# Edge attention pass of a fused graph transformer: per-tile sums kept in two PSUM banks instead of folding the SBUF accumulator into every item

## The chip, the cores and the metric

One core of one Trainium2 chip. The metric is the device time of one execution of the whole program, in microseconds, as the median of several runs.

## The reference, cut to what matters

The program runs a whole two-layer model on 3125 nodes and 100000 edges. The change lies in the edge attention of the second layer:

```python
def _edge_attention(xn, edge_index, ef, ew, Wq, bq, Wk, bk, Wv, bv, We, be, Wo, bo):
    n = xn.shape[0]
    scale = DH ** (-0.5)
    q = (xn @ Wq + bq).reshape(n, H, DH)
    k = (xn @ Wk + bk).reshape(n, H, DH)
    v = (xn @ Wv + bv).reshape(n, H, DH)
    src, dst = (edge_index[0], edge_index[1])
    ep = ef @ We + be
    scores = jnp.einsum('ehd,ehd->eh', q[dst], k[src] + ep[:, None, :]) * scale
    scores = scores * ew[:, None]
    m = jax.ops.segment_max(scores, dst, num_segments=n)
    m = jnp.where(jnp.isfinite(m), m, 0.0)
    ex = jnp.exp(scores - m[dst])
    s = jax.ops.segment_sum(ex, dst, num_segments=n)
    attn = ex / s[dst]
    out = jax.ops.segment_sum(attn[:, :, None] * v[src], dst, num_segments=n)
    out = out.reshape(n, D) @ Wo + bo
    return out
```

H is 8 heads and DH is 32. `dst` is sorted, so the edges of one node, and of one tile of 128 nodes, stand together.

## The kernel before

The edges are cut into 416 items of 256 edges; all edges of an item end in the same tile of 128 nodes (25 tiles), and a table `sh.tile_id` says which. `stage_flash` takes 8 items at a time: one window, 52 windows in all, each of four groups of two items. The loop is software-pipelined: one pass of `body(s, a, ffn)` works on the scores of window `s` (the next one) and on the sums of window `a` (the one before it), and on a piece of an unrelated feed-forward (`ffn`) that fills TensorE. Every engine runs its own written-out list in order; semaphores tie them together. No planner is involved.

For window `s` and each group `g`:

- GpSimd gathers the key and value rows of the edges (`store<-kv_d`, L2816) into a ring of two windows; it may overwrite a group's rows only when `sums_done` says that the sums of two windows before are through.
- ScalarE's `place(s, g)` makes the one-hot matrix `mem_t` in two passes (L2945, L2948); TensorE's `ask(s, g)` multiplies it with the queries into the one `query` bank pair (L2840, 8 instructions of 256 columns: each fp32 product is two instructions). VectorE's `add` (L3038), `mult` (L3045) and `reduce` (L3049) turn this into scores, and `scale` (L3055) ends the window. `ask(s, g)` waits for `mult(s, g-1)`, since `query` is a single buffer.

For window `a`:

- TensorE turns the scores (L2868), VectorE scans them for the running maxima (`within`, L3065 on; `across`, L3075 on), with small TensorE products in between (L2884, L2890), then TensorE turns the result back (L2901, L2902) and ScalarE takes the exponential (L2985).
- VectorE's `rescale` (L3105) multiplies the accumulator of the window's first tile by the fall of the maximum, and `weigh(a, g)` (L3110) multiplies the value rows by the weights.
- ScalarE's `belong(a, g)` (L2954, L2957) makes the one-hot matrices `member`; TensorE's `collect(a, n)` (L2853) sums item `n` into one of three PSUM banks, `n % 3`, with four instructions of 264 columns.
- TensorE's `fold(a, n)` (L2860) then adds the SBUF accumulator of the item's tile by a product with the identity, two instructions of 264 columns. ScalarE's `keep(a, n)` (L2963) copies the bank back to the accumulator. `fold(n)` waits for `keep(n-1)`; `collect` itself waits for a `keep` only in items 0 and 1.

In the text, A0 to A3 are `ask(s, 0)` to `ask(s, 3)`, and C0 to C3 the collecting of the items 2g and 2g+1 of window `a`. TensorE's list before, from the middle of a pass, is A1, items 0, 1, 2, 3 with the folds of 0 to 2, A2, fold 3, items 4, 5 with fold 4, A3, fold 5, items 6, 7 with their folds. ScalarE's list there is keep 0, place 2, keep 1, belong 2, keep 2, place 3, keep 3, belong 3, keep 4, place 0 of the next window, keep 5 to 7.

Of the kernel before, what the change touches and what calls it, by code (L numbers as in the profile page):

```python
# [319 lines left out]
def stage_edge_tables(nc, sh):  # L320

    with ExitStack() as ctx:
# [65 lines left out]
        with nc.Block() as block:  # L388
            @block.sync
            def _(sp):  # L390
# [8 lines left out]
                sp.dma_start(sh.tile_id[:, 0:NI], sh.tile_d.rearrange("(a i) -> a i", a=1)).then_inc(ids_in, 16)  # L399
# [2249 lines left out]
def stage_flash(nc, sh, w1, w2, b1):  # L2649
# [6 lines left out]
    with ExitStack() as ctx:  # L2656
# [42 lines left out]
        pa = sb("pa", [P, P + H])  # L2699
        query = ps("query", [P, 4 * D])  # L2700
# [40 lines left out]
        down_added = sem("down_added")  # L2741

        def tile_numbers(eng, w):

            _, values = nc.values_load_multi_w_load_instructions(
                sh.tile_id[0:1, bass.ds(WI * w.at, WI)], engines=[eng.engine], min_val=0, max_val=NT - 1,
                skip_runtime_bounds_check_because="the table was clamped to 0 .. NT - 1 when it was made")
            return values
# [13 lines left out]
        with nc.Block() as block:  # L2762
# [62 lines left out]
            def _(pe):  # L2825
# [18 lines left out]
                def collect(a, n):  # L2844

                    g = n // 2
                    pe.wait_ge(member_ready, G * a.at + (g + 1))
                    pe.wait_ge(pv_ready, G * a.at + (g + 1))
                    if n < 2:
                        pe.wait_ge(added, WI * a.at + (n + 1))  # L2850
                    for k in range(SUBS):
                        c = n % 2 * SUBS + k
                        pe.matmul(sums[:, n % 3, 0:W], member[:, g % 2, c, :], ring[:, a.side * WS + 4 * g + c, HI_],  # L2853
                                  start=(k == 0), stop=False)

# [706 lines left out]
```

## Time and profile before

| what | value |
|---|---|
| median of 3 runs | 3732.68 us (3732.53 to 3735.69) |
| profiled execution, its own time | 3734.78 us |
| its span | 3733.0 us |
| mean granted TensorE clock | 0.878 |
| edge attention pass (`stage_flash`) | about 1900 to 3227 us of the span |

The profile is of one execution. "Busy" of TensorE counts pipelined matmuls with modelled ends, so rows of several matmuls give the time from the first start to the last end; the time that a group really takes from the engine is the distance from its start to the start of the next group. PE is TensorE, PEld its weight loads, DVE VectorE, ACT ScalarE, POOL GpSimd.

### The profile page before, as it was taken

The page shows a single profiled execution, that of the slowest core. Times are in us where ns is not written, and L with a number is a line of the kernel's source. Part 1 is how long each engine was busy: PE and PEld are TensorE (multiplying, and loading weights), DVE is VectorE, ACT ScalarE, POOL GpSimd, SP SyncE. Part 2 cuts the span into 40 slices and gives each one's busy share as a digit, 9 for nine tenths or more (in the row PEclk, how much of TensorE's full clock was granted, in tenths as well). Part 3 has the DMA queues.
Part 4 walks back from the last instruction along what each step waited for, and adds up shares of the span by engine and source line. Part 5 has one row for each costly group of instructions (what it writes and reads, how often), then busy time and mean ns, then how long its engine had stood idle before and what let it go on. Part 6 is the DMA issues. An engine that isn't in the chain of part 4 may idle for free. (4 is left out here: it accounts for less than half of the span.)

```text
span 3733.0 us, 52272 instructions
## 1 busy us (share of the span) xinstructions
PE 3127.7 (84%) x13504; PEld 2408.8 (65%) x13504; DVE 2161.4 (58%) x4835; ACT 1687.2 (45%) x3903; POOL 1888.5 (51%) x1845
## 2 busy tenths in 40 slices
PE   2778888788878689769859999999999999659798
PEld 2567666566665578646437777777777777436565
DVE  6333334333334600075569999999999999653515
ACT  1444333333334122233246676667676676332323
POOL 2777777777772044401046666666666666120010
PEclk8778767777778599979769999999999999779899
DMA  5555555555550167641067777777777777300000
GB/s 143 148 147 146 139 153 140 154 144 142 147 141 20 44 192 218 182 167 63 9 190 218 222 219 218 214 224 218 218 216 221 221 219 209 111 24 1 22 5 35
DMA packets 345535, 547.29 MB, mean 147 GB/s; under 512 B 170928, under 2 KB 222389, under 8 KB 344967
## 3 DMA queue, kind: packets, MB, share of 16 engines
q0 software_dynamic: 113216, 348.74, 32.8%
q1 hardware_dynamic: 224312, 183.42, 16.8%
q10 hardware_dynamic: 7743, 12.07, 1.0%
q8 instruction: 111, 1.82, 0.2%
q14 instruction: 153, 1.25, 0.1%
HBM read 493.32 MB, written 51.90 MB: 146 GB/s over the span
## 5 line engine op out<-in xcount | busy, mean ns | idle before, releaser
L2816 POOL DMA_INDIRECT store<-kv_d,src_of x832 | 872.4, 1049 | 414.6 <-issue 242.1
L821 POOL DMA_INDIRECT agg_rows<-xn_d,src_of x832 | 800.0, 962 | 268.7 <-issue 242.3
L993 PE MATMUL agg_sums<-agg_rows,agg_member 128*128 128x257 f32 x1664 | 578.0, 501 | 181.7 <-DVE acc L885 92.4
L834 ACT ACTIVATE agg_rows<-agg_rows,weight_of 128x256 f32<-128x256 f32 x832 | 373.0, 500 | 632.1 <-DMA agg_rows<-xn_d,src_of 631.5
L993 PEld LDWEIGHTS agg_sums<-agg_rows,agg_member 128*128 128x128 f32 x1664 | 387.7, 249 | 323.9 <-DVE acc L885 130.0
L885 DVE TENSOR_TENSOR acc<-acc,agg_sums 128x257 f32 x416 | 176.3, 424 | 598.9 <-PE agg_sums L993 598.0
L2840 PE MATMUL flash_query<-q,flash_mem_t 128*128 x1664 | 411.7, 391 | 48.3 <-DVE store L3045 37.7
L2853 PE MATMUL flash_sums<-store,flash_member 128*128 128x264 f32 x1664 | 422.8, 387 | 2.2 <-DVE store L3110 2.2
L2840 PEld LDWEIGHTS flash_query<-q,flash_mem_t 128*128 128x128 f32 x1664 | 312.7, 193 | 100.9 <-issue 54.6
L2853 PEld LDWEIGHTS flash_sums<-store,flash_member 128*128 128x128 f32 x1664 | 317.1, 191 | 56.1 <-issue 2.2
L3045 DVE TENSOR_TENSOR store<-store,flash_query 128x1024 f32<-128x1024 f32 x208 | 252.3, 1213 | 39.3 <-PE flash_query L2840 39.0
L2963 ACT ACTIVATE acc<-flash_sums 128x264 f32 x416 | 159.3, 383 | 252.2 <-PE flash_sums L2860 251.8
L2860 PE MATMUL flash_sums<-acc,ident 128*128 x832 | 269.2, 405 | 2.1 <-ACT acc L2963 1.6
L983 PEld LDWEIGHTS agg_edge<-agg_we,agg_feats 65*128 65x128 f32 x1664 | 249.7, 230 | 23.8 <-issue 10.4
L2954 ACT ACTIVATE flash_member<-lane,lane_of 128x128 f32<-128x128 f32 x832 | 264.1, 395 | 0.1
L3038 DVE TENSOR_TENSOR store<-store,flash_ep 128x1024 f32<-128x1024 f32 x208 | 252.5, 1214 | 9.9 <-DMA flash_ep<-ep_d 9.5
L3110 DVE TENSOR_TENSOR store<-store,flash_pa 128x1056 f32<-128x1056 f32 x208 | 255.7, 1251 | 0.0
L983 PE MATMUL agg_edge<-agg_we,agg_feats 65*128 65x32 f32 x1664 | 239.8, 304 | 11.6 <-DMA agg_feats<-in_ef_t_dram 11.0
L3049 DVE TENSOR_REDUCE flash_dots<-store 128x32 f32<-128x1024 f32 x208 | 247.8, 1211 | 1.8
L2860 PEld LDWEIGHTS flash_sums<-acc,ident 128*128 128x128 f32 x832 | 145.4, 189 | 64.3 <-issue 48.7
L876 DVE TENSOR_SCALAR agg_member<-lane,lane_of 128x128 f32<-128x128 f32 x832 | 175.8, 300 | 10.1 <-issue 1.5
L1649 DVE TENSOR_TENSOR moe_y<-moe_down,moe_b 128x512 f32<-128x512 f32 x32 | 22.1, 692 | 244.9 <-PE moe_down L1508 244.9
(468 smaller groups left out, 4574.3 us busy)
## 6 DMA issues: line engine op xcount, KB each, us to landing
moe_w<-in_L_ffn_W_dram SPq DMA_DIRECT2D x64, 512.0 KB
agg_feats<-in_ef_t_dram SPq DMA_DIRECT2D x104, 256.0 KB, 4.4
flash_goal<-goal_d SPq DMA_DIRECT2D x52, 512.0 KB, 4.4
agg_rows<-xn_d,src_of POOLq DMA_INDIRECT x832, 2.8
ep_d<-agg_ep SPq DMA_DIRECT2D x52, 256.0 KB
store<-kv_d,src_of POOLq DMA_INDIRECT x832, 4.1
flash_ep<-ep_d SPq DMA_DIRECT2D x416, 32.0 KB
flash_flags<-flags_d SPq DMA_DIRECT2D x416, 32.0 KB
```

The costliest lines, as they stand in the source:

```text
L821: pool.indirect_dma_start(rows[:, q, 0:D], None, sh.xn_d, bass.IndirectOffsetOnAxis(ap=sh.src_of[:, c:c + 1], axis=0)).then_inc(gathered[u ...
L834: act.activation(rows[:, q, 0:D], rows[:, q, 0:D], ACT.Copy, scale=sh.weight_of[:, bass.ds((UI * i + u) * SUBS + k, 1)]).then_inc(weighted, 1)
L983: last = pe.matmul(edge[:, p, c * DH:(c + 1) * DH], feats[:, p, c * P:(c + 1) * P], we_s[:, :], start=True, stop=True)
L993: last = pe.matmul(sums[:, j % 4, 0:W], member[:, c % (2 * BI * SUBS), :], rows[:, c % NB, :], start=(c % SUBS == 0), stop=(c % SUBS == SU ...
L2816: pool.indirect_dma_start(ring[:, s, :], None, sh.kv_d, bass.IndirectOffsetOnAxis(ap=sh.src_of[:, c:c + 1], axis=0)).then_inc(gathered[p][ ...
L2840: last = pe.matmul(query[:, c * D:(c + 1) * D], mem_t[:, g % 2, c * P:(c + 1) * P], sh.q[:, bass.ds(t, 1), :], start=True, stop=True)
L2853: pe.matmul(sums[:, n % 3, 0:W], member[:, g % 2, c, :], ring[:, a.side * WS + 4 * g + c, HI_], start=(k == 0), stop=False)
L2860: pe.matmul(sums[:, n % 3, 0:W], sh.ident[:, :], sh.acc[:, bass.ds(tiles[n], 1), :, :].rearrange("p a h v -> p (a h v)"), start=False, sto ...
L2954: act.activation(member[:, g % 2, k, :], sh.lane[:, :], ACT.Abs, scale=-1.0, bias=sh.lane_of[:, bass.ds(WS * a.at + (4 * g + k), 1)])
L3038: dve.tensor_tensor(r, r, ep[:, s.side, 4 * g:4 * g + 4, :].unsqueeze(2).to_broadcast([P, 4, H, DH]), ALU.add).then_inc(add_done, 1)
L3045: dve.tensor_tensor(r, r, query[:, :].rearrange("p (k f) -> p k f", k=4), ALU.mult).then_inc(mult_done, 1)
L3110: dve.tensor_tensor(r, r, e.unsqueeze(3).to_broadcast([P, 4, H, VW]), ALU.mult).then_inc(pv_ready, 1)
```

## The change

The two items of a group are summed straight into a running sum that stays in PSUM. Bank 1 or 2 of `sums` belongs to a tile, by turns (`bank_id`); the next tile takes the other bank. There is no fold. Where an item is the first of its tile, its bank must first forget what it holds: a product of one row and one column of zeros (`clear_l`, `clear_r`, bf16) with `start=True` goes to column 511 of the bank that `open_id` names; where the item is not the first, `open_id` is 0 and the product goes to the unused bank 0. `keep` still copies the bank to the SBUF accumulator after every item, `rescale` now works on the PSUM bank, and VectorE makes both tables from `tile_id` at the start of the stage. The order of the calls on TensorE and ScalarE and their waits change too.

```diff
-                def collect(a, n):
-
-                    g = n // 2
+                def collect(a, g, banks, opened):
                     pe.wait_ge(member_ready, G * a.at + (g + 1))
                     pe.wait_ge(pv_ready, G * a.at + (g + 1))
-                    if n < 2:
-                        pe.wait_ge(added, WI * a.at + (n + 1))
-                    for k in range(SUBS):
-                        c = n % 2 * SUBS + k
-                        pe.matmul(sums[:, n % 3, 0:W], member[:, g % 2, c, :], ring[:, a.side * WS + 4 * g + c, HI_],
-                                  start=(k == 0), stop=False)
-
-                def fold(a, n, tiles):
-
-                    pe.wait_ge(rescaled, a.at + 1)
-                    pe.wait_ge(added, WI * a.at + (n + 2))
-                    pe.matmul(sums[:, n % 3, 0:W], sh.ident[:, :],
-                              sh.acc[:, bass.ds(tiles[n], 1), :, :].rearrange("p a h v -> p (a h v)"),
-                              start=False, stop=True).then_inc(sums_done, 1)
+                    if g == 0:
+                        pe.wait_ge(rescaled, a.at + 1)
+                    if WI * a.at + 2 * g > 0:
+                        pe.wait_ge(added, WI * a.at + 2 * g)
+                    for n in (2 * g, 2 * g + 1):
+                        pe.matmul(sums[:, bass.ds(opened[n], 1), 511:512].rearrange("p a w -> p (a w)"), clear_l[:, :], clear_r[:, :],
+                                  start=True, stop=True)
+                        for k in range(SUBS):
+                            c = n % 2 * SUBS + k
+                            last = pe.matmul(running(banks[n]), member[:, g % 2, c, :], ring[:, a.side * WS + 4 * g + c, HI_],
+                                             start=False, stop=(k == SUBS - 1), skip_group_check=True)
+                        last.then_inc(sums_done, 1)
...
-                        tiles = tile_numbers(pe, a)
-                        collect(a, 0)
-                        fold(a, 0, tiles)
-                        collect(a, 1)
-                        fold(a, 1, tiles)
-                        collect(a, 2)
-                        collect(a, 3)
-                        fold(a, 2, tiles)
+                        banks, opened = bank_numbers(pe, a), open_numbers(pe, a)
+                        collect(a, 0, banks, opened)
                     if s is not None:
                         ask(s, 2, ask_tiles)
                     if a is not None:
-                        fold(a, 3, tiles)
-                        collect(a, 4)
-                        collect(a, 5)
-                        fold(a, 4, tiles)
+                        collect(a, 1, banks, opened)
                     if s is not None:
                         ask(s, 3, ask_tiles)
                     if a is not None:
-                        fold(a, 5, tiles)
-                        collect(a, 6)
-                        fold(a, 6, tiles)
-                        collect(a, 7)
-                        fold(a, 7, tiles)
+                        collect(a, 2, banks, opened)
+                        collect(a, 3, banks, opened)
+                    else:
+                        pe.wait_ge(banks_ready, 1)
...
-                def keep(a, n, tiles):
-                    act.wait_ge(sums_done, WI * a.at + (2 * WI + n + 1))
+                def keep(a, n, tiles, banks):
+                    act.wait_ge(sums_done, WI * a.at + (2 * WI + n // 2 * 2 + 2))
+                    if n % 2 == 1:
+                        act.wait_ge(added, WI * a.at + n)
                     act.activation(sh.acc[:, bass.ds(tiles[n], 1), :, :].rearrange("p a h v -> p (a h v)"),
-                                   sums[:, n % 3, 0:W], ACT.Copy).then_inc(added, 1)
+                                   running(banks[n]), ACT.Copy).then_inc(added, 1)
...
-                        keep(a, 3, tiles)
+                        keep(a, 3, tiles, banks)
                         belong(a, 3)
-                        keep(a, 4, tiles)
                     if more:
                         place(after(s), 0)
                     if a is not None:
-                        for n in range(5, WI):
-                            keep(a, n, tiles)
+                        for n in range(4, WI):
+                            keep(a, n, tiles, banks)
...
-                dve.sem_inc(added, 2)
...
-                def rescale(a, tile):
+                def rescale(a, bank):
                     dve.wait_ge(exp_ready, a.at + 2)
-                    dve.wait_ge(added, WI * a.at + 2)
-                    r = sh.acc[:, bass.ds(tile, 1), :, :].rearrange("p a h v -> p (a h) v")
+                    if a.at > 0:
+                        dve.wait_ge(added, WI * a.at)
+                    r = running(bank).rearrange("p (h v) -> p h v", h=H)
```

TensorE's list in one pass, from the last product of the turn back (`flash_diag`) on; `flash_query` is the output of an ask and `flash_sums` that of a collect or a fold. Before:

```order
L2902 MATMUL flash_small<-flash_diag,flash_first_hot 128x8
L2840 ISA
L2840 MATMUL flash_query<-q,flash_mem_t 128x256 x2
L2840 ISA
L2840 MATMUL flash_query<-q,flash_mem_t 128x256 x2
L2745 TENSOR_LOAD tile_id
L2853 MATMUL flash_sums<-store,flash_member 128x264 x2
L2860 ISA
L2860 MATMUL flash_sums<-acc,ident 128x264
L2853 MATMUL flash_sums<-store,flash_member 128x264 x2
L2860 ISA
L2860 MATMUL flash_sums<-acc,ident 128x264
```

The same place now, as far as the start of A2:

```order
L2917 MATMUL flash_small<-flash_diag,flash_first_hot 128x8
L2859 ISA
L2859 MATMUL flash_query<-q,flash_mem_t 128x256 x2
L2859 ISA
L2859 MATMUL flash_query<-q,flash_mem_t 128x256 x2
L2752 TENSOR_LOAD tile_id x2
L2871 ISA
L2871 MATMUL flash_sums<-flash_clear_r,flash_clear_l 128x1
L2875 ISA
L2875 MATMUL flash_sums<-store,flash_member 128x264 x2
```

Two products of a collect and one of a fold have become one clearing product and two of a collect, each behind a register instruction (ISA), and a second table is read (TENSOR_LOAD). What follows the second item moved most: A2 stood behind four items, it now stands behind two, and A3 behind four in place of six.

VectorE's list at the start of the stage has these rows new, behind the last one that it had there before:

```order
L3040 CAST flash_member<-tile_id 1x416
L3041 MEMSET flash_hidden 1x1
L3042 MEMSET flash_member 1x416
L3044 TENSOR_TENSOR flash_hidden<-flash_member 1x415
L3046 SCALAR_TENSOR_TENSOR flash_member<-flash_hidden,flash_member 1x416
L3048 CAST tile_id<-flash_member 1x416
L3050 TENSOR_SCALAR tile_id<-tile_id 1x416
L3052 CAST flash_member<-tile_id 1x416
L3054 TENSOR_SCALAR flash_member<-flash_member 1x416
L3056 TENSOR_TENSOR flash_hidden<-flash_hidden,flash_member 1x416
L3057 CAST tile_id<-flash_member 1x416
L3059 CAST tile_id<-flash_hidden 1x416
```

They run once and stand ahead of the first `add`, where nothing stood before; a clearing of the three `sums` banks also joins the memsets ahead of them.

## Rows read from the trace of the kernel before

**Rows 1.** The page: span in 40 slices, TensorE, VectorE and granted clock.

```profile
PE   2778888788878689769859999999999999659798
...
DVE  6333334333334600075569999999999999653515
...
PEclk8778767777778599979769999999999999779899
```

**Rows 2.** Busy time by stretch, one of 260 us in the pass.

```profile
2220.00:2480.00 260.00, 247.88 (x1177) 200.24 (x1176) 241.48 (x366) 180.68 (x433) 175.47 (x167) 1.00 0.75 218
```

**Rows 3.** VectorE's waits between 1960 and 3200 us: total, times, longest.

```profile
DVE store L3045 <- PE flash_query L2840: 32.7, 51, 1.1
DVE flash_run L3075 <- PE flash_small L2884: 16.0, 50, 0.3
```

**Rows 4.** Timeline of one window: start, us, engine, line, count, idle before.

```profile
2503.09 1.89 PE L2840 MATMUL flash_query<-q,flash_mem_t 128*128 x8
...
2504.81 0.61 PE L2860 MATMUL flash_sums<-acc,ident 128*128 x2
...
2505.26 1.21 DVE L3045 TENSOR_TENSOR store<-store,flash_query 128x1024 f32<-128x1024 f32 x1
...
2508.20 0.32 PE L2868 MATMUL flash_small<-ident,flash_scaled 128*128 128x128 f32 x1
...
2508.35 1.96 PE L2877 MATMUL flash_up<-flash_xt,store 128*128 128x128 f32 x16
...
2509.13 0.41 DVE L3065 TENSOR_TENSOR_SCAN flash_ahead<-flash_flags,flash_small 128x128 f32<-128x128 f32 x1
...
2510.53 0.23 PE L2884 MATMUL flash_small<-flash_z,flash_row_head 128*8 128x32 f32 x2 [0.21 <-DVE flash_z L3070]
...
2514.92 1.21 DVE L3045 TENSOR_TENSOR store<-store,flash_query 128x1024 f32<-128x1024 f32 x1
...
2516.38 1.99 PE L2840 MATMUL flash_query<-q,flash_mem_t 128*128 x8 [0.68 <-DVE store L3045]
...
2518.21 1.05 PE L2853 MATMUL flash_sums<-store,flash_member 128*128 128x264 f32 x4
...
2519.10 0.61 PE L2860 MATMUL flash_sums<-acc,ident 128*128 x2
...
2519.84 0.39 ACT L2963 ACTIVATE acc<-flash_sums 128x264 f32 x1 [1.86 <-PE flash_sums L2860]
...
2520.87 0.72 ACT L2948 ACTIVATE flash_mem_t<-flash_mem_t,ones 128x512 f32<-128x512 f32 x1
...
2523.24 1.89 PE L2840 MATMUL flash_query<-q,flash_mem_t 128*128 x8
...
2525.24 1.22 DVE L3045 TENSOR_TENSOR store<-store,flash_query 128x1024 f32<-128x1024 f32 x1 [0.62 <-PE flash_query L2840]
```

**Rows 5.** The page: the group of the folds, all windows.

```profile
L2860 PE MATMUL flash_sums<-acc,ident 128*128 x832 | 269.2, 405 | 2.1 <-ACT acc L2963 1.6
```

**Rows 6.** Timeline of an earlier stage, around a matmul of one column.

```profile
1704.05 0.28 PE L2170 MATMUL mid_zsum<-ones,mid_kr 128*128 128x1 f32 x2
1704.19 0.68 PE L2168 MATMUL mid_zsum<-store,mid_kr 128*128 128x256 f32 x2
```

**Rows 7.** The table read: duration ns, first and last start.

```profile
L2745 PEldq TENSOR_LOAD <-tile_id x104: 587/591/634, 1909.2 to 3208.2; - x104
```

**Rows 8.** VectorE at the start of the pass (timeline), and an operation on 257 elements (page).

```profile
1917.97 2.36 DVE L3038 TENSOR_TENSOR store<-store,flash_ep 128x1024 f32<-128x1024 f32 x2 [9.53 <-DMA flash_ep<-ep_d]
...
L885 DVE TENSOR_TENSOR acc<-acc,agg_sums 128x257 f32 x416 | 176.3, 424 | 598.9 <-PE agg_sums L993 598.0
```

**Rows 9.** TensorE at its slower clock: by stretch, and twice in the timeline.

```profile
460.00:720.00 260.00, 212.62 (x867) 164.63 (x867) 98.06 (x340) 97.39 (x227) 197.83 (x205) 0.74 0.56 150
...
515.56 2.05 PE L993 MATMUL agg_sums<-agg_rows,agg_member 128*128 128x257 f32 x4 [2.28 <-issue]
...
1931.50 3.62 PE L2840 MATMUL flash_query<-q,flash_mem_t 128*128 x8 [2.67 <-DVE store L3045]
```

More of the change, by code:

```diff
@@ L2741, in stage_flash, with numbers, bank_numbers, open_numbers @@
         down_added = sem("down_added")
-        def tile_numbers(eng, w):
[L2745 to L2748, printed above, removed]
+        banks_ready = sem("banks_ready")
+        def numbers(eng, w, table, least, most):
+            _, values = nc.values_load_multi_w_load_instructions(
+                table[0:1, bass.ds(WI * w.at, WI)], engines=[eng.engine], min_val=least, max_val=most,
+                skip_runtime_bounds_check_because="the table was made on the chip within these bounds")
+            return values
+        def tile_numbers(eng, w):
+            return numbers(eng, w, sh.tile_id, 0, NT - 1)
+        def bank_numbers(eng, w):
+            return numbers(eng, w, bank_id, 1, 2)
+        def open_numbers(eng, w):
+            return numbers(eng, w, open_id, 0, 2)
+        def running(bank):
+            return sums[:, bass.ds(bank, 1), 0:W].rearrange("p a w -> p (a w)")
         def after(s):
@@ L2982, in body @@
                         belong(a, 0)
-                        tiles = tile_numbers(act, a)
+                        tiles, banks = tile_numbers(act, a), bank_numbers(act, a)
                         act.wait_ge(back_ready, a.at + 1)
@@ L2986, in body @@
                         belong(a, 1)
-                        keep(a, 0, tiles)
+                        keep(a, 0, tiles, banks)
                     if s is not None:
@@ L2990, in body @@
                     if a is not None:
-                        keep(a, 1, tiles)
+                        keep(a, 1, tiles, banks)
                         belong(a, 2)
-                        keep(a, 2, tiles)
+                        keep(a, 2, tiles, banks)
                     if s is not None:
@@ L3002, in body @@
                     if a is not None:
-                        for n in range(5, WI):
-                            keep(a, n, tiles)
+                        for n in range(4, WI):
+                            keep(a, n, tiles, banks)
+                    else:
+                        act.wait_ge(banks_ready, 1)
                 windows(act, body)
@@ L3009, in _ @@
             def _(dve):
-                dve.sem_inc(added, 2)
                 dve.sem_inc(down_added, 1)
+                dve.memset(clear_l[:, :], 0.0)
+                dve.memset(clear_r[:, :], 0.0)
+                dve.memset(sums[:, :, :], 0.0)
                 dve.memset(sh.acc[:, :, :, :], 0.0)
@@ L3028, in _ @@
                 dve.drain().then_inc(heads_ready, 1)
+                dve.tensor_copy(turns, sh.tile_id[0:1, :])
+                dve.memset(opens[:, 0:1], 1.0)
+                dve.memset(none, 0.0)
+                dve.drain()
+                dve.tensor_tensor(opens[:, 1:NI], turns[:, 1:NI], turns[:, 0:NI - 1], ALU.not_equal)
+                dve.drain()
+                dve.tensor_tensor_scan(turns, opens, none, 0.0, ALU.add, ALU.max)
+                dve.drain()
+                dve.tensor_copy(bank_id[:, :], turns)
+                dve.drain()
+                dve.tensor_scalar(bank_id[:, :], bank_id[:, :], 1, None, ALU.bitwise_and)
+                dve.drain()
+                dve.tensor_copy(turns, bank_id[:, :])
+                dve.drain()
+                dve.tensor_scalar(turns, turns, 1.0, None, ALU.add)
+                dve.drain()
+                dve.tensor_tensor(opens, opens, turns, ALU.mult)
+                dve.tensor_copy(bank_id[:, :], turns)
+                dve.drain()
+                dve.tensor_copy(open_id[:, :], opens)
+                dve.drain().then_inc(banks_ready, 1)
                 def key_rows(s, g):
```

14 lines of the change are left out of this document (10 added, 4 removed).

## Prediction

> **What bounds the kernel now.** The slices say where the change lies: TensorE and VectorE are both at 9 tenths for the whole edge pass, about a third of the span, and the granted clock is full there, which it is hardly anywhere else for so long [rows 1]. A stretch inside the pass says how near both are: 247.9 and 241.5 us busy of 260 [rows 2]. So neither can win much without the other. VectorE's waits tell who waits for whom: 32.7 us of its idle time end with an ask (`mult` waits for the query product), 51 times, and 16.0 us with the small product L2884 [rows 3]. That is 0.64 and 0.32 us of each window. The timeline then gives one period: from `mult` 2 at 2525.24, back over its wait of 0.62 us for A2, to `mult` 0 at 2514.92, whose end lets A1 start. Behind A1, TensorE has four items and three folds before A2 [rows 4]. The loop that sets the time is thus `mult` 0, A1, collects and folds, A2, `mult` 2, VectorE's list, `mult` 0. The same `mult` 2 stood at 2500.69 one window earlier (2525.24 less the 24.55 us that I take as the period; 51 such periods make up the pass).
>
> **What goes.** A window has 16 fold instructions of 264 columns (832 in all [rows 5]). A collect of four starts at 2518.21 and its fold at 2519.10 [rows 4], so one instruction takes 0.2225 us of TensorE, and the folds 3.56 us of the window.
>
> **What comes.** Eight clearing products a window, each with its own weights and one column. The nearest row is L2170: two instructions of one column in an earlier stage go from 1704.05 to the next at 1704.19, so 0.07 us each [rows 6], the lower bound. Above stands 0.23, the whole of the small pair L2884 from first start to last end; half of it, 0.12, is what one of two such products takes with a start of its own [rows 4]. A register instruction now stands ahead of each, so I take c = 0.12 us rather than 0.07: 0.96 a window. The second table read takes 0.59 us on TensorE's sequencer [rows 7]; it is issued while A1's 1.83 us run, and two of 0.59 still fit, so I cost it at nothing (0.6 us a window if that cover were gone). `rescale` keeps its 264 elements; PSUM or SBUF, `add` and `mult` differ by nothing in the rows (1.22 and 1.21 us), so nothing. By TensorE's load alone the window would shrink by 3.56 - 0.96 = 2.60 us.
>
> The tables: 11 operations on 416 elements of one row. An operation on 257 takes 0.42 us, so 416 take about 0.7, and the scan, 0.41 for 128 elements [rows 4], at most 1.3; with the PSUM memset some 9 to 10 us. VectorE sits idle 9.53 us before its first `add` [rows 8]. Cost 0 to 1 us, once; I take 0.
>
> **What moves: the waits.** This is where I expect the time. `collect` of group g now waits for every earlier `keep`, and `keep` waits for the whole pair. Between the asks this makes one chain that hands over between TensorE and ScalarE. I follow it from `mult` 0 (time 0 = 2514.92), with three lengths from [rows 4]: an ask holds TensorE 1.73 us (2503.09 to 2504.81); a pair of items needs 1.05 + 0.89 = 1.94 us to its last end and holds TensorE 1.78, each plus 2c; from that end to `keep` there are 0.13 us (2519.71 to 2519.84).
> - A1 starts at 1.46 and C0 at 3.29, as now. C0 ends at 5.23 + 2c. `keep` 0 starts at 5.36 + 2c. `place` 2 stands behind it and is ready 1.75 later (2519.84 to 2520.87 + 0.72), at 7.11 + 2c; A2 starts at 7.24 + 2c, in place of 8.32. So A2 comes 0.84 us earlier and `mult` 2's wait of 0.62 goes.
> - C1 starts at 8.97 + 2c and ends at 10.91 + 4c. `keep` 2 was through before A2's end; now it waits for C1, and `place` 3 behind it: 12.79 + 4c. A3 starts at 12.92 + 4c, in place of 12.72 (2503.09 is one period earlier). TensorE is idle for about 2.2 us. `mult` 3 follows at 14.92 + 4c against 14.89 (2505.26): the whole gain at `mult` 2 is given back.
> - C2 starts at 14.65 + 4c, ends at 16.59 + 6c. `keep` 4 starts at 16.72 + 6c, `keep` 5 must wait for it, 0.43, and ends at 17.54 + 6c. C3 waits for `keep` 5: 17.67 + 6c, and TensorE is idle 1.1 us again.
> - The turn L2868 stands behind C3: 19.45 + 8c. Now it stands at 17.83 (2508.20). It is 1.62 + 8c late.
> - Next late is L2884. VectorE's list reaches it 1.40 after L3065, which can start some 0.38 after the turn; TensorE has 16 instructions of the feed-forward between (2508.35 to 2510.31) and gets to it about 2.15 us after the turn, now 2.33. So it is late by 1.44 + 8c, and from there to the next `mult` 0 the list is VectorE's and does not change.
>
> With c = 0.12 a window is 2.40 us longer, with 0.07 2.00 and with 0.23 3.28. Times 51: 122 us (102 to 167). GpSimd is not behind this: its 16 gathers of about 1.3 us need 21 us of what is then 27.
>
> **The clock.** The pass has the full clock now. The stage with the lower mean, 0.74, has TensorE idle in pieces of one to two us between its groups [rows 9]; four instructions behind an idle piece of 2.28 us took 2.05 us there, where the pass needs 1.05 for four. In the pass itself, an ask behind 2.67 us of idle time took 3.62 us, against 1.99 [rows 9, 4]. The new window has two idle pieces of about 2.2 us (before A2 and before A3) and one of 1.1. So I expect the lower of the two levels (1.2 in place of 2.4 GHz) now and then: one group of eight a window at 3.62 in place of 1.99, 1.63 us, and since TensorE is on the chain nearly all the way, all of it counts: 83 us. Bounds: nothing, and two groups a window, 166 us.
>
> The Trainium skill ("TensorE: Matmul & The Clock Gate", the section on a second failure mode, PSUM-queue depth cycling) speaks against this change in the same way: a kernel that cycles through PSUM banks and leaves TensorE small idle pieces between groups goes back and forth between the two levels. By that rule the pass would lose its full clock; by the slice row alone (1.00 throughout) one would add nothing. The rows of the earlier stage agree with the rule.
>
> **The sum.** The profiled execution took 3734.78 us, span 3733.0, the runs' median 3732.68: they agree within 0.1%, so I add to the median. 3732.7 + 122 + 83 = 3938 us.
>
> **The rivals.**
> - *Chain without clock loss.* The hand-overs cost as worked out, but the pieces of 2.2 us are too short to lower the clock: 3855 us (3835 to 3900 by c). For it: the pass has idle pieces of 0.7 us every window and stays at 1.00. Against: the rows at 2.28 and 2.67 us. Chance 0.33; the forecast with clock loss has 0.43.
> - *More is lost.* Two groups or more a window at the lower clock, or c above 0.3: 4021 us and more. Chance 0.07 beyond 4040.
> - *The gain at A2 stands* (other side). If `place` 3 did not end up behind C1, that is if A3 could start by 12.72 - 0.62 = 12.1 and C3 could follow C2 without a stop, `mult` 2's wait is all that changes: 51 times 0.62, 32 us, so 3701 us; VectorE's whole wait for TensorE, 50 us, would be the floor, 3683. It decides at the point where `keep` 2 and `keep` 4, 5 cost TensorE less than the 2.6 us that the folds free. For it: TensorE's load falls by 2.6 us. Against: ScalarE's list has `keep` 2 ahead of `place` 3, and C1 is behind A2. Chance 0.12.
> - *Nothing to be seen.* The two cancel within 0.2%: 0.03. A small loss up to 3825: 0.02.
>
> **How the numbers follow.** The likeliest is 3938 us. The range goes from the chain with the smallest c and no clock loss, 3835, rounded down to 3825, to two groups a window plus a little, 4035; it leaves out the other side and the excess. About 0.2% (7.5 us) is what a measurement of this kernel can tell from no change. Faster 0.12, same 0.03, slower 0.85.
>
> **What would show it.** In the changed profile: the waits of TensorE for `keep` (ACT acc) and `place` (ACT flash_mem_t) new, of about 1 and 2 us, once and twice a window; VectorE waiting about 1 us or more for L2868 or L2884 and for A3, and no longer for A2; a window of 27 to 29 us; TensorE's instructions of the pass fewer by 416; the granted clock of the pass below 1.00. I am wrong in the chain if A3 does not wait for `place` 3; wrong in the clock term if the pass keeps 1.00; wrong in c if a pair of items holds TensorE much more or less than 2.0 us.

## The result, and the profile after

The change makes the kernel slower: 4036.14 us (median of 4 runs, 4033.61 to 4038.53) against 3732.61 us before (3731.63 to 3735.69, 4 runs). The ratio is 1.0811 [1.0797, 1.0825], a loss of 303.5 us. The forecast was 3938 us with a range of 3825 to 4035 us, so the time lies 1 us above the range and 98 us above the forecast.

The page of the changed kernel, its slices (to be held against [rows 1]), and two groups of its part 5:

```profile
PE   2888878888885996895778778877877787649888
...
DVE  6323333433345001746777777777777777562524
...
PEclk8777777877785998996899999999999999869999
...
L2859 PE MATMUL flash_query<-q,flash_mem_t 128*128 x1664 | 500.8, 453 | 255.2 <-ACT flash_mem_t L2953 217.5
...
L2871 PEld LDWEIGHTS flash_sums<-flash_clear_r,flash_clear_l 1*128 1x128 bf16 x416 | 38.0, 91 | 245.0 <-issue 245.0
```

TensorE and VectorE, both at 9 tenths in the edge pass before, are both at 7 to 8 tenths now: neither of them bounds the pass any longer; they wait for something. The busy times of the same stretch as in [rows 2] say it in microseconds (TensorE, its weight loads, VectorE, ScalarE, GpSimd, then the granted clock): TensorE has 42 us less of 260, VectorE 43 less, and the granted clock is 0.93:

```profile
2220.00:2480.00 260.00, 206.16 (x874) 145.41 (x872) 198.85 (x299) 143.29 (x345) 140.09 (x135) 0.93 0.61 175
```

The waits of VectorE and TensorE between 2000 and 3450 us (total, times, longest) name it. Against [rows 3], VectorE's wait for an ask has grown from 32.7 to 192.7 us, twice a window, and a wait for the turn (L2883, L2868 before) is new. TensorE in turn waits for `place` (L2953) twice a window and for `keep` (L2970) once:

```profile
DVE store L3077 <- PE flash_query L2859: 192.7, 94, 4.4
DVE flash_ahead L3097 <- PE flash_small L2883: 105.5, 47, 2.5
...
PE flash_query L2859 <- ACT flash_mem_t L2953: 192.7, 94, 2.1
PE flash_sums L2871 <- ACT acc L2970: 66.1, 47, 1.4
```

The timeline of one window (the changed kernel, 2517 to 2544 us) shows the chain, from the last part of one pass into the next (start, duration, engine, line, count, idle before):

```profile
2517.66 0.39 ACT L2970 ACTIVATE acc<-flash_sums  x1 [1.07 <-PE flash_sums L2875]
...
2518.26 0.39 ACT L2970 ACTIVATE acc<-flash_sums  x1 [0.21 <-ACT acc L2970]
...
2518.91 0.17 PE L2871 MATMUL flash_sums<-flash_clear_r,flash_clear_l 1*128 1x1 bf16 x1 [1.41 <-ACT acc L2970]
...
2521.22 0.27 PE L2883 MATMUL flash_small<-ident,flash_scaled 128*128 128x128 f32 x1
...
2521.59 0.42 DVE L3097 TENSOR_TENSOR_SCAN flash_ahead<-flash_flags,flash_small 128x128 f32<-128x128 f32 x1 [2.43 <-PE flash_small L2883]
...
2527.47 1.21 DVE L3077 TENSOR_TENSOR store<-store,flash_query 128x1024 f32<-128x1024 f32 x1
...
2528.94 1.99 PE L2859 MATMUL flash_query<-q,flash_mem_t 128*128 x8 [0.68 <-DVE store L3077]
...
2531.07 0.17 PE L2871 MATMUL flash_sums<-flash_clear_r,flash_clear_l 1*128 1x1 bf16 x1
...
2532.27 0.09 PEld L2871 LDWEIGHTS flash_sums<-flash_clear_r,flash_clear_l 1*128 1x128 bf16 x1 [0.34 <-issue]
2532.27 0.17 PE L2871 MATMUL flash_sums<-flash_clear_r,flash_clear_l 1*128 1x1 bf16 x1
2532.37 0.74 PEld L2875 LDWEIGHTS flash_sums<-store,flash_member 128*128 128x128 f32 x4
2532.38 1.16 PE L2875 MATMUL flash_sums<-store,flash_member 128*128 128x264 f32 x4
...
2533.69 0.39 ACT L2970 ACTIVATE acc<-flash_sums  x1 [3.16 <-PE flash_sums L2875]
...
2534.72 0.72 ACT L2953 ACTIVATE flash_mem_t<-flash_mem_t,ones 128x512 f32<-128x512 f32 x1
...
2535.58 3.65 PE L2859 MATMUL flash_query<-q,flash_mem_t 128*128 x8 [2.05 <-ACT flash_mem_t L2953]
...
2541.78 0.39 ACT L2970 ACTIVATE acc<-flash_sums  x1 [4.10 <-PE flash_sums L2875]
...
2543.67 1.99 PE L2859 MATMUL flash_query<-q,flash_mem_t 128*128 x8 [2.05 <-ACT flash_mem_t L2953]
```

Read from 2531.07 on: C0 ends, `keep` 0 starts, `place` 2 follows, and only then A2, after 2.05 us in which TensorE has nothing. A2 itself takes 3.65 us instead of the 1.99 of a group of eight at the full clock. The same hand-over comes again between C1 and A3 (2541.78 to 2543.67), and a smaller one between C2 and C3, at the top.

The length of a window is best read from turn to turn, the first and the last of the 52 turns. Before, of two timelines of L2868:

```profile
1938.17 0.33 PE L2868 MATMUL flash_small<-ident,flash_scaled 128*128 128x128 f32 x1 [3.04 <-DVE flash_scaled L3055]
...
3202.58 0.28 PE L2868 MATMUL flash_small<-ident,flash_scaled 128*128 128x128 f32 x1
```

After, of L2883:

```profile
1937.74 0.30 PE L2883 MATMUL flash_small<-ident,flash_scaled 128*128 128x128 f32 x1 [3.09 <-issue]
...
3503.95 0.27 PE L2883 MATMUL flash_small<-ident,flash_scaled 128*128 128x128 f32 x1
```

That is 1264.41 us for 51 periods before, 24.79 each, and 1566.21 now, 30.71 each. The pass accounts for 301.8 of the 303.5 us; outside it nothing moved. The setup of the tables on VectorE stayed in its idle time, as predicted: the first turn is even 0.4 us earlier.

### The profile page after: what moved, and what is told of

Its sections match the earlier page's. It is cut to its first block and busy times, and to the rows that moved or that the text cites. A ratio compares the mean times of both kernels' runs of the same rounds, so it can differ in the third digit from the quotient of the medians.

```text
span 4036.8 us, 51618 instructions
## 1 busy us (share of the span) xinstructions
PE 3180.7 (79%) x13088; PEld 2331.4 (58%) x13088; DVE 2177.5 (54%) x4850; ACT 1687.8 (42%) x3903; POOL 1882.3 (47%) x1845
## 5 line engine op out<-in xcount | busy, mean ns | idle before, releaser
L2859 PE MATMUL flash_query<-q,flash_mem_t 128*128 x1664 | 500.8, 453 | 255.2 <-ACT flash_mem_t L2953 217.5
L2859 PEld LDWEIGHTS flash_query<-q,flash_mem_t 128*128 128x128 f32 x1664 | 350.3, 221 | 358.2 <-issue 303.3
L2875 PE MATMUL flash_sums<-store,flash_member 128*128 128x264 f32 x1664 | 500.4, 425 | 0.3
L2970 ACT ACTIVATE acc<-flash_sums x416 | 160.3, 385 | 613.6 <-PE flash_sums L2875 591.3
L2875 PEld LDWEIGHTS flash_sums<-store,flash_member 128*128 128x128 f32 x1664 | 294.6, 197 | 39.0 <-issue 0.2
L2871 PEld LDWEIGHTS flash_sums<-flash_clear_r,flash_clear_l 1*128 1x128 bf16 x416 | 38.0, 91 | 245.0 <-issue 245.0
L2962 ACT ACTIVATE flash_member<-flash_member,ones 128x512 f32<-128x512 f32 x208 | 150.1, 722 | 14.3
```

The source lines that it names most:

```text
L2859: last = pe.matmul(query[:, c * D:(c + 1) * D], mem_t[:, g % 2, c * P:(c + 1) * P], sh.q[:, bass.ds(t, 1), :], start=True, stop=True)
L2875: last = pe.matmul(running(banks[n]), member[:, g % 2, c, :], ring[:, a.side * WS + 4 * g + c, HI_], start=False, stop=(k == SUBS - 1), sk ...
```

## Experiments

Below, "the length of a window" is always taken as above, from the first to the last turn, divided by 51, and the "quiet" length is the lower quartile of the 51 periods (24.59 us in the kernel before). "Slow asks" are groups of eight of L2859 (L2840 in the kernel before) of over 2.1 us in place of 1.99, counted from the first to the last turn; the kernel before has 2 of them, the changed kernel has 62, of which 49 are an A2. All traces are of one execution each.

### First set

Four kernels went to a chip on which the kernel before took 4408.72 us itself. The traces there show stops of some 10 us in which ScalarE and VectorE stand still together, for instance in the timeline of the first of them:

```profile
2840.37 1.14 ACT L2985 ACTIVATE flash_hidden<-flash_up,flash_b 128x128 f32<-128x128 f32 x4 [9.42 <-DMA xn_d<-store]
2840.41 0.23 DVE L3107 TENSOR_TENSOR_SCAN flash_run<-flash_steps,flash_run,flash_small 8x16 f32<-8x16 f32 x1 [10.39 <-remote]
```

The times of this set (4591.11, 4545.97, 4557.58 and 4593.78 us) are therefore no measure, and three of the four were run again on another chip. Their expectations:

The places ahead of the keeps in ScalarE's list:

> ScalarE makes place 2 and place 3 ahead of keep 0 and keep 2; nothing else changes. Theory H (hand-overs): the two idle pieces of TensorE of 2.05 us before A2 and A3 vanish, and with them the slower clock (A2 back from 3.65 to about 1.9 us). What stays is the 1.4 us before C3. By the durations of the changed kernel's trace the window becomes about 25.6 us in place of 30.54: 51 times 4.9 less, about 3785 us. Theory O (TensorE's own overhead, that is clearing products and register instructions, carries the loss): the same work stands on TensorE, so at most 50 us are won: 3985 us or more.

Three unused products ahead of A2 and of A3:

> Three more products of 256 columns with the identity (into the unused bank 0, 1.3 us) stand on TensorE ahead of A2 and of A3, inside the idle pieces of 2.05 us. They compute nothing that is used. Theory C (clock): TensorE's idle pieces shrink to about 0.8 us, the slower clock does not come, A2 takes 1.9 in place of 3.65 us: the kernel gets faster with more work, by 51 times 1.75 us, to about 3945 us, clock 1.00 in the pass. If the clock falls for another reason: the same 4036 us or up to 4060, since the products only fill idle time.

No clearing products:

> The eight clearing products of a window, with their register instructions, are left out, so the sums of different tiles run together (that part of the computation is missing). If each costs the 0.31 us that the changed trace shows between its start and that of its item, 2.48 us of a window go and the time is about 3910 us. If it costs the 0.12 us of the prediction, 0.96 us go: 3987 us. If other waits hide it: 4036 us.

The clearing products at a fixed address, so that no register instruction stands ahead of them:

```diff
-                        pe.matmul(sums[:, bass.ds(opened[n], 1), 511:512].rearrange("p a w -> p (a w)"), clear_l[:, :], clear_r[:, :],
-                                  start=True, stop=True)
+                        pe.matmul(sums[:, 0, 511:512], clear_l[:, :], clear_r[:, :], start=True, stop=True)
```

> The clearing products stay but go to bank 0 always, a fixed address, so the register instruction ahead of each is gone (the forgetting of the right bank is missing). If the register instruction is the cost, the time is near that of the kernel without clears (3910 us). If the product with its own weights is the cost, it is near 4036 us.

This one needs no time to be read, only the distance of two items in an undisturbed window of its timeline:

```profile
2525.01 0.17 PE L2871 MATMUL flash_sums<-flash_clear_r,flash_clear_l 1*128 1x1 bf16 x1
...
2526.19 0.09 PEld L2871 LDWEIGHTS flash_sums<-flash_clear_r,flash_clear_l 1*128 1x128 bf16 x1 [0.34 <-issue]
2526.20 0.17 PE L2871 MATMUL flash_sums<-flash_clear_r,flash_clear_l 1*128 1x1 bf16 x1
```

1.19 us from item to item, as in the changed kernel (2531.07 to 2532.27, 1.20): the computed address is not what a clearing product costs.

### The places first

ScalarE's list alone is written in another order; no work is added or removed.

```diff
                         belong(a, 1)
-                        keep(a, 0, tiles, banks)
                     if s is not None:
                         place(s, 2)
                     if a is not None:
+                        keep(a, 0, tiles, banks)
                         keep(a, 1, tiles, banks)
-                        belong(a, 2)
-                        keep(a, 2, tiles, banks)
                     if s is not None:
                         place(s, 3)
                     if a is not None:
+                        belong(a, 2)
+                        keep(a, 2, tiles, banks)
                         keep(a, 3, tiles, banks)
```

> The kernel of the run places first again, since there the kernel before took 4409 us in place of 3733, with stalls of up to 10 us of ScalarE and VectorE together that neither kernel has in the first profiles. If TensorE's two idle pieces of about 2 us and the slower clock carry the loss, as theory H says: about 3785 us beside 3733 for the kernel before, clock 1.00 in the pass. If TensorE's own overhead carries it: 3985 us or more.

Measured: 3771.99 us (3768.78 to 3776.99), ratio to before 1.0109 [1.0093, 1.0126]. Of the 303.5 us of loss 264 are gone. Its timeline at the place where the changed kernel has the hand-over:

```profile
2506.99 0.72 ACT L2953 ACTIVATE flash_mem_t<-flash_mem_t,ones 128x512 f32<-128x512 f32 x1
...
2508.02 1.16 PE L2875 MATMUL flash_sums<-store,flash_member 128*128 128x264 f32 x4
...
2509.01 1.89 PE L2859 MATMUL flash_query<-q,flash_mem_t 128*128 x8
...
2509.33 0.39 ACT L2970 ACTIVATE acc<-flash_sums  x1 [1.61 <-PE flash_sums L2875]
```

`place` 2 is through before C0 ends, A2 follows C0 with no idle time, and `keep` 0 runs beside it. The granted clock of the pass is back at full speed:

```profile
2220.00:2480.00 260.00, 227.41 (x1062) 165.79 (x1061) 233.76 (x366) 175.78 (x423) 193.84 (x165) 1.00 0.73 212
```

The window is 25.50 us long, with one slow ask. It follows that the order "keep, then place" in ScalarE's list makes most of the loss, and that the clock is lost by way of it. VectorE no longer waits for any ask between 2000 and 3200 us; what it still waits for is small products of TensorE, the turn above all, 1.28 us a window:

```profile
DVE flash_ahead L3097 <- PE flash_small L2883: 60.1, 47, 1.5
```

### Work put into the gaps

```diff
                     if s is not None:
+                        if a is not None:
+                            for n in range(3):
+                                pe.matmul(sums[:, 0, 0:D], sh.ident[:, :], sh.q[:, 0, :], start=True, stop=True)
                         ask(s, 2, ask_tiles)
```

and the same ahead of `ask(s, 3)`: twelve instructions of 256 columns more in each window, into the unused bank 0.

> The kernel with six more instructions of 256 columns ahead of A2 and of A3 again, for the same reason. Theory C (idle pieces lower the clock): about 3945 us and clock 1.00 in the pass. If the clock has another cause: 4036 to 4060 us and a slow A2 as before.

Measured: 3955.47 us (3954.23 to 3959.28), 1.0603 [1.0585, 1.0621]. With more work and nothing else changed it is 81 us faster than the changed kernel. Its timeline around A2:

```profile
2503.42 1.46 PE L2926 MATMUL flash_sums<-q,ident 128*128 128x256 f32 x6
...
2505.64 1.99 PE L2859 MATMUL flash_query<-q,flash_mem_t 128*128 x8 [0.75 <-ACT flash_mem_t L2959]
```

And the busy times and the clock of its stretch:

```profile
2220.00:2480.00 260.00, 226.77 (x1034) 165.90 (x1034) 205.26 (x318) 152.19 (x367) 151.72 (x143) 0.99 0.65 185
```

A2 still waits for `place`, but the idle piece is 0.75 us long in place of 2.05, and the ask is back at 1.99 us. One of its asks is slow in place of 62. The window is 29.08 us long, 28.73 in the quiet ones: this is the chain with the clock loss all but taken out. So the changed kernel's window of 30.71 us splits into 24.79, the chain and the clock. By the quiet length the chain makes 3.94 us and the clock 1.98; by the mean of 29.08 they make 4.29 and 1.63. The second split compares like with like, since the 24.79 is a mean too. The slow asks alone, each less 1.99, add up to 82 us, 1.6 a window.

### Without the clearing products

The product of L2871 is left out, and with it the read of the table `open_id`, which nothing on TensorE uses then (104 table reads there in place of 156). Nothing else is changed.

> The kernel without the clearing products again (the forgetting of a bank is left out). At 0.31 us each: about 3910 us. At the 0.12 us of the prediction: 3987 us.

Measured: 3866.5 us (3861.53 to 3870.45), 1.036 [1.0343, 1.0377], 170 us under the changed kernel and 44 under the lower of the two values expected. The waits of 2.05 us for `place` are all still there, so the hand-over stays. The window is 27.41 us, 26.40 in the quiet ones, and 28 asks are slow in place of 62. Against the quiet 28.73 of the kernel above, eight clearing products are worth 2.33 us, 0.29 each (some 0.1 us of the 2.33 may be the table read); the distance of two items says 0.31 (1.20 less 0.89 for four products [rows 4]). Of the 170 us some 119 are this difference (51 times 2.33); the rest goes with the fewer slow asks.

The same run closes a rival. A pair without its clears takes 1.94 us, the 1.05 + 0.89 of [rows 4], though both items now add to a running sum at a computed address:

```profile
2522.32 1.94 PE L2873 MATMUL flash_sums<-store,flash_member 128*128 128x264 f32 x8
```

So neither the shared bank nor the register address of the items costs TensorE anything here; the 0.31 us are the clear.

The 264 us of the order and the 170 us of the clears add up to more than the loss of 303.5, so they overlap. Both take in part of the clock loss, and the clears ahead of A2 and A3 can cost time only while VectorE waits for these asks.

### Three edits: places first, tables early, clears in pairs

To the reordered list come two edits on TensorE: the tables are read ahead of the wait for L2916, and both clearing products of a pair stand ahead of both items.

```diff
+                        banks, opened = bank_numbers(pe, a), open_numbers(pe, a)
                         pe.wait_ge(p_ready, a.at + 1)
...
-                        banks, opened = bank_numbers(pe, a), open_numbers(pe, a)
                         collect(a, 0, banks, opened)
...
                     for n in (2 * g, 2 * g + 1):
                         pe.matmul(sums[:, bass.ds(opened[n], 1), 511:512].rearrange("p a w -> p (a w)"), clear_l[:, :], clear_r[:, :],
                                   start=True, stop=True)
+                    for n in (2 * g, 2 * g + 1):
                         for k in range(SUBS):
```

> Places first, and two more edits: the two tables are read into TensorE's registers before the turn back instead of right ahead of C0, and both clearing products of a pair stand ahead of both items. Against places first I expect 0.3 us a window less for the tables, and 4 times 0.3 us less if the 0.31 us of a clearing product are a stop between items, which now falls once a pair: 51 times 1.5 us, about 3785 - 77 = 3708 us. If each clearing product stops the weight loads wherever it stands, only the tables gain: 3770 us.

Measured: 3751.32 us (3749.13 to 3755.64), 1.0056 [1.004, 1.0073]: 21 us better than the places alone, where 77 was hoped for. What a pair of clears costs now is in its timeline:

```profile
2502.23 0.11 PEld L2871 LDWEIGHTS flash_sums<-flash_clear_r,flash_clear_l 1*128 1x128 bf16 x2 [0.33 <-issue]
2502.23 0.20 PE L2871 MATMUL flash_sums<-flash_clear_r,flash_clear_l 1*128 1x1 bf16 x2
2502.36 2.05 PE L2876 MATMUL flash_sums<-store,flash_member 128*128 128x264 f32 x8
```

The two products go by in 0.13 us and the stop of the weight loads comes once in place of twice. Less came of it in time because VectorE is nearly the bound again (238.96 us busy of 260 in the stretch, [rows 2] has 241.48). With the places first it waited for no ask any more, so time saved ahead of A2 and A3 is not seen. Only its wait for the turn could shrink: it went from 1.28 us a window to 0.88, and the window from 25.50 to 25.14. TensorE mostly waits for VectorE:

```profile
DVE flash_ahead L3098 <- PE flash_small L2884: 43.1, 49, 2.1
...
PE flash_query L2859 <- DVE store L3078: 107.7, 96, 1.6
PE flash_sums L2871 <- ACT acc L2971: 73.1, 52, 1.4
```

One hand-over of the changed kernel is left, C3 behind `keep` 5, and it still makes VectorE wait for the turn.

### The two small edits alone, and clears of another kind

These three start from the changed kernel again. First the tables read ahead of the wait for L2916, as in the diff above:

> The changed kernel, with the two tables read into TensorE's registers ahead of the turn back, where TensorE waits for VectorE anyway, in place of right ahead of C0. If the second read holds C0 back by 0.3 us (C0 starts 3.60 us after mult 0, predicted 3.29): 51 times 0.3, about 4020 us. If it is hidden, as the prediction said: 4036 us. A shift of the idle pieces against the clock could hide or double this.

Measured: 4040.13 us (4038.93 to 4044.94), 1.082 [1.0802, 1.0838]. C0 now starts 1.92 us after A1 in 50 of 51 windows. In the changed kernel the median is 1.98 us, with single windows above 2.05, such as the one shown (2528.94 to 2531.07, 2.13). So the read held C0 up by 0.06 us as a rule, and in time that is worth nothing. The median period fell from 30.37 to 30.25 us, while 64 asks are slow in place of 62.

Then both clearing products of a pair ahead of both items, as in the diff above:

> The changed kernel, with both clearing products of a pair ahead of both items. The run with three edits shows the pair at 1.9 to 2.0 us of TensorE in place of 2.4. So four times 0.4 us a window: 51 times 1.6, about 3954 us; nothing if other waits take it up: 4036 us.

Measured: 3984.47 us (3972.53 to 3991.13), 1.0662 [1.0637, 1.0687], 52 us under the changed kernel, where 82 was hoped for. The window is 29.75 us, 28.08 in the quiet ones, with 56 slow asks. Against the quiet 28.73 with the filled gaps that is 0.65 us a window, 0.16 a pair in place of the 0.4 expected; A2 starts 6.33 us after A1 in place of 6.50 (medians). The rest of the 52 us goes with the fewer slow asks.

The third clears with full-size operands, the identity as weights and a column of zeros of 128 rows in fp32, which is two instructions:

```diff
-        clear_r = sb("clear_r", [1, 1], BF16)
+        clear_r = sb("clear_r", [P, 1])
...
-                        pe.matmul(sums[:, bass.ds(opened[n], 1), 511:512].rearrange("p a w -> p (a w)"), clear_l[:, :], clear_r[:, :],
+                        pe.matmul(sums[:, bass.ds(opened[n], 1), 511:512].rearrange("p a w -> p (a w)"), sh.ident[:, :], clear_r[:, :],
                                   start=True, stop=True)
```

> The clearing product uses the 128 x 128 identity and a column of 128 zeros in fp32 in place of one row of bf16 weights and one bf16 zero: two instructions in place of one. If the 0.31 us are a stop because weights of one row and bf16 can't be loaded while products of 128 rows run, it now costs 2 times 0.07 us as in the stage where the price was taken from: 8 times 0.16 less, 51 times 1.3, about 3970 us. If any clearing product (a register address, another bank) stops the loads: 4036 us or somewhat more.

Measured: 4038.08 us (4033.83 to 4039.08), 1.0807 [1.0789, 1.0825], no change. Its timeline shows a clear of another shape:

```profile
2536.85 0.41 PEld L2871 LDWEIGHTS flash_sums<-flash_clear_r,ident 128*128 128x128 f32 x2
2537.07 0.28 PE L2871 MATMUL flash_sums<-flash_clear_r,ident 128*128 128x1 f32 x2
```

The load starts 0.22 us ahead of its product, with no stop of 0.34 before it: here the load was pulled ahead under the product that ran. But there are two instructions, and together they take 0.23 us: items stand 1.12 us apart (2535.95 to 2537.07), less the 0.89 of four products. That is 0.08 less than in the changed kernel. So the time is that of the second case expected, but not for its reason: the stop did go, and two instructions took most of its place. The quiet window is 0.21 us shorter (30.08 against 30.29), 66 asks are slow in place of 62, and the mean of 30.65 is all but the 30.71 of the changed kernel. Whether a few more slow asks are the rule when the window gets a little shorter, here and with the tables early, and why, stays open: there is one trace of each.

### The last pair behind the next turn

To the three edits: the 16 feed-forward instructions of a pass move ahead of its turn, and C3 of the pass before is held back until both are issued; its keeps stand behind the activation of the hidden layer. The lines on TensorE that hold C3 back:

```diff
+                    if left:
+                        collect(*left.pop())
                     if s is not None:
                         ask_tiles = tile_numbers(pe, s)
...
-                        collect(a, 3, banks, opened)
+                        left.append((a, 3, banks, opened))
```

> The three edits, and C3 moves behind the next window's turn L2868 (keep 6 and 7 behind the hidden layer's activation), while the 16 instructions of the feed-forward move ahead of the turn into the idle 1.4 us where TensorE waited for keep 5. The turn then no longer stands behind C3: VectorE's wait of 1.0 us for it goes, 51 times 1.0 to 1.1 us: about 3697 us against 3751, that is below the kernel before (3733). If the feed-forward ahead of the turn makes it late again (C2 ends 1.8 us before the scores are ready): 3740 us.

Measured: 3739.36 us (3730.95 to 3745.87, 10 runs), 1.0013 [1.0004, 1.0023]: level with the kernel before. Its waits:

```profile
DVE store L3085 <- DMA store<-kv_d,src_of: 29.7, 35, 2.0
...
DVE store L3092 <- PE flash_query L2859: 10.3, 14, 1.5
```

The wait for the turn is gone from VectorE's list. A new one is there: `add` waits for gathered rows. The likely reason is argued and was not tried by itself: GpSimd may overwrite a group's rows only when `sums_done` says that C3 is through, and C3 now ends later. The expectation had named 3740 us for another case, a turn that comes late again, which the trace does not show; that this number came out is luck. The quiet windows of this version take 24.06 us, 0.53 less than those of before (24.59), but the mean is 24.89, with 15 slow asks, all of them an A1. So no version measured here beats the kernel before. One whose mean lay as near its quiet length as that of the kernel before would take 3732.6 - 51 x 0.53 = 3706 us by this estimate, and it was not found.

## Why the prediction was right in direction and wrong in size

**The chain was right.** The forecast had the period grow by 1.44 + 8c. With the clock loss taken out the quiet period is 28.73, which is 3.94 above the 24.79 that the forecast started from, and with c = 0.31 the formula gives 3.92. Without clearing products (c = 0) it gives 24.79 + 1.44 = 26.23, and 26.40 was measured. Held against the quiet 24.59 of the kernel before, the growth is 4.14 and 1.81 us, so the formula falls short by 0.2 to 0.4 us a window, 10 to 20 us in all; the fit to 0.02 is in part luck. Step by step in the timeline above, with `mult` 0 at 2527.47 as time 0: A2 at 8.11 (7.24 + 2c, 7.86 with c = 0.31; from A1 on, 6.50 in the median where the formula has 6.40), A2 and A3 both behind `place`, `keep` 5 0.60 us behind `keep` 4 (0.43) and C3 behind it, idle pieces of 2.05, 2.05 and 1.41 us (2.2, 2.2 and 1.1), L2899 1.99 us behind the turn (2.15). TensorE's waits that were to show it are there in kind and number: `place` twice a window, `keep` once. One sign failed: VectorE was to wait no longer for A2, and it does so in every window, 1.6 us in the mean. Most of that is the slow A2; with the gaps filled it is 0.4, since with two clears at 0.31 A2 comes too late anyway. Its other signs follow: a window of 30.7 us where 27 to 29 was named, and pairs that hold TensorE 2.4 us and not 2.0, which the prediction had named as what would show c to be wrong. That `place` stuck behind `keep` is the cause was shown by the reordered list, which took back 264 us.

**The step that failed is the price of a clearing product.** It was taken as 0.12 us, with 0.07 and 0.23 as bounds; it is 0.31 by the distance of two items and 0.29 by leaving them out. At 51 windows and eight products that is 51 x 8 x 0.19 = 78 us of the 98 that the forecast was short of. The other 20 us lie in the chain or in the clock, depending on which of the two splits above is taken. What the traces show at this place is in the weight loads. The load of the second clearing product of a pair has an idle piece of 0.34 us before it (2532.27), where the later loads of a collect start 0.22 us ahead of their own products. (The 245.0 us over all 416 loads also hold other waits, such as that for `keep` 5.) The row for this was in the trace of the kernel before, and was not read; the small product L2890 there, with weights of 8 rows, behind an ask:

```profile
2512.66 0.29 PEld L2890 LDWEIGHTS flash_small<-flash_carry,flash_head_row 8*128 8x128 f32 x2 [0.33 <-issue]
```

The rows taken instead, L2170 and L2884 [rows 6, 4], gave the duration of such a product, but not the stop ahead of it. The address from a register, the reason given for 0.12 over 0.07, is no part of it. Whether it is the one row or the bf16 that keeps the load from being pulled ahead no run tells apart, since the full-size clear changed both; the load of L2890 has 8 rows in fp32 and the same stop, which speaks for the rows.

**The clock term was right, or a little small.** One group of eight a window at 3.62 in place of 1.99 was forecast, 83 us. There are 62 slow asks in 51 windows, 3.31 us each in the mean, and they lose 82 us. Of the 303.5 us the chain makes 201 to 219 and the clock 101 to 83, by the two splits above. That it is about one slow group a window was a guess between none and two, and no rule behind it was tested. The rival without clock loss (3855) is out. The rival that came is "more is lost", with "c above 0.3" as one of its two conditions; it had a chance of 0.07 for a time beyond 4040, and the time lies just short of that. The Trainium skill ("TensorE: Matmul & The Clock Gate", the section on a second failure mode, PSUM-queue depth cycling) has TensorE go back and forth between the two levels when small idle pieces come between its groups: the trace agrees, with full clock before, 0.93 now with pieces of 2.05 us twice a window, and 0.99 with the same chain and pieces of 0.75 us. The piece of 1.41 us ahead of C3 is in the changed kernel and in the one with the places first, and the latter has 1.00.

**The table read was costed at nothing, and that held.** Its cover is thinner than forecast: in the window shown the two reads take 0.60 and 0.76 us, and C0 is held up there (2.13 us after A1 against 1.92). As a rule the delay is 0.06 us, and moving the reads gained no time. `rescale` on PSUM (0.44 us against 0.43) and the tables on VectorE were right at nothing.

**The range** never took the upper bound of c and the upper bound of the clock together. With c = 0.23 they reach 3732.7 + 167 + 166 = 4066 and would have held the time, without the right price for c.

**Where the gain went.** The folds' 3.56 us a window did leave TensorE, and clearing products took 8 x 0.31 = 2.48 of it back, so the change frees 1.1 us and not 2.6. That could be won only as far as VectorE lets it, which was idle 0.96 us of a window for TensorE [rows 3]. Against it stand the hand-overs.

## What to carry to other kernels

When one engine both empties a result buffer and prepares the next operand of the engine that fills it, follow its list in order: the preparation belongs ahead of the emptying, or each coarser wait becomes a hand-over (here 264 us by order alone). Count the idle pieces that a change leaves on TensorE, since they can also cost the clock (here two of 2.05 us a window did), and unused products in the gap can pay (81 us here). Price a small product by the distance between its neighbours in a timeline where it stands between large ones, the idle time of the weight loads included, not by its own duration.

## What the runs showed of the hardware that was not expected

- A product with weights of one row has its weight load stand still for 0.33 to 0.34 us behind a product of 128 rows, with a computed address or a fixed one; two such products in a row have the stop once. A load of 128 rows in fp32 at the same place starts 0.22 us ahead of its product.
- Adding twelve instructions of 256 columns to a window, 2.9 us of TensorE (two times 1.46), made it 1.63 us shorter (30.71 to 29.08).
- A shorter chain does not always give a shorter pass: with 0.1 and 0.2 us less in the median and the quiet window there were 64 and 66 slow asks in place of 62 (one trace each), and the time stayed the same within 0.1%.
